# Layer 0's output projection as seven block products with streamed weight forms

## What is computed

```python
# layer 0: 6 heads of 128
q = _heads(seq_inputs @ Wq + bq)
k = _heads(seq_inputs @ Wk + bk)
v = _heads(seq_inputs @ Wv + bv)
scores = jnp.einsum('bhqd,bhkd->bhqk', q, k) / np.sqrt(HEAD_SIZE)
probs = jax.nn.softmax(scores + bias, axis=-1)      # bias: 0 or -9e15 by adj
ctx = jnp.einsum('bhqk,bhkd->bhqd', probs, v)
return ctx @ Wf + bf
# layer 1: 12 heads of 64, logits from tanh(h), leaky, masked, softmax
h = jnp.einsum('bnd,ade->bane', feat_in, W)
feat_out = jax.nn.elu(jnp.einsum('banm,bame->bane', attn, h) + b)
gate = jax.nn.sigmoid(feat_in @ H_w.T + H_b)
return gate * feat_out + (1.0 - gate) * feat_in
```

## Time and profile before

| What | Value |
|---|---|
| Median of 3 runs | 2498.94 us |
| Profiled execution, span from its first to its last instruction | 2497.4 us |
| PE busy | 2466.8 us, 99% |
| DVE busy | 1987.7 us, 80% |
| ACT, POOL busy | 922.8 us (37%), 785.2 us (31%) |
| One iteration of the loop (Q0 at 1149.84 us to the next Q0 at 1226.06 us) | 76.22 us |
| HBM read and written | 67.03 MB, 25.17 MB |

### The profile page before, as it was taken

How to read it: one execution, slowest core, us unless ns; L and a number is a source line. 1 busy time by engine, 2 the same in 40 slices (tenths; PEclk the granted TensorE clock), 3 DMA queues, 4 the chain that set the end, 5 groups by cost and what they waited for, 6 DMA issues and landing times.

```text
span 2497.4 us, 54938 instructions
## 1 busy us (share of the span) xinstructions
PE 2466.8 (99%) x22921; PEld 1765.1 (71%) x22952; DVE 1987.7 (80%) x2748; ACT 922.8 (37%) x1146; POOL 785.2 (31%) x558
## 2 busy tenths in 40 slices
PE   7999999999999999999999999999999999999997
PEld 6676677776777766777766777667777667776676
DVE  7878878778777788787787777887877877778868
ACT  6433333233333333333343333333333433333334
POOL 0133332333332333323333323333233333233331
PEclk9999999999999999999999999999999999999999
DMA  7344343343343443433433434434434334344332
GB/s 260 90 83 78 75 94 84 74 95 69 82 101 73 85 79 76 92 85 74 93 71 80 101 76 82 81 75 90 87 77 88 73 79 101 76 82 82 76 65 52
DMA packets 544290, 214.66 MB, mean 86 GB/s; under 512 B 509825, under 2 KB 519041, under 8 KB 544257
## 3 DMA queue, kind: packets, MB, share of 16 engines
q1 hardware_dynamic: 544256, 214.18, 39.8%
HBM read 67.03 MB, written 25.17 MB: 37 GB/s over the span
## 4 chain that ended last, share of the span: by engine, by line
PE 95%; DVE 3%; ACT 1%; issue 1%; DMA 0%; POOL 0%; SPq 0%; DVEq 0%; ACTq 0%; POOLq 0%
PE pair_prj L613 58%; PE pair_prj L637 29%; PE pair_att L653 3%; PE pair_att L734 2%; PE pair_att L750 1%; PE pair_att L793 1%; DVE w_lo L1005 1%; DMA arena<-in_L_gnn_Wq 0%; PE pair_prj L663 0%; ACT w_hi L1580 0%; PE pair_prj L779 0%; DVE w_top L967 0%; ACT w_lo L1615 0%; DVE arena L1055 0%; DVE p_place L1326 0%
## 5 line engine op out<-in xcount | busy, mean ns | idle before, releaser
L613 PE MATMUL pair_prj<-w_hi,arena 128*128 128x512 f16 (+1 forms) x6168 | 1445.5, 325 | 0.9 <-DVE w_lo L1005 0.9
L613 PE MATMUL pair_prj<-w_lo,arena 128*128 128x512 f16 (+1 forms) x3084 | 1002.8, 325 | 0.0
L613 PEld LDWEIGHTS pair_prj<-w_hi,arena 128*128 128x128 f16 x6168 | 603.4, 98 | 398.6 <-DVE w_lo L1005 1.0
L637 PE MATMUL pair_prj<-arena,w_hi 128*128 128x256 f16 x4536 | 747.8, 273 | 1.0 <-issue 1.0
L637 PE MATMUL pair_prj<-arena,w_lo 128*128 128x256 f16 x2268 | 618.2, 273 | 0.0
L637 PEld LDWEIGHTS pair_prj<-arena,w_hi 128*128 128x128 f16 x4536 | 439.6, 98 | 51.4 <-issue 1.4
L613 PEld LDWEIGHTS pair_prj<-w_lo,arena 128*128 128x128 f16 x3084 | 301.8, 98 | 192.7
L1911 POOL TENSOR_TENSOR rstd<-var_eps,minus_half 128x2 f32<-128x2 f32 x62 | 62.1, 1002 | 652.0 <-DVE var_eps L1024 645.0
L637 PEld LDWEIGHTS pair_prj<-arena,w_lo 128*128 128x128 f16 x2268 | 221.9, 98 | 25.7
L1930 POOL TENSOR_TENSOR arena<-arena,b_row 128x768 f32<-128x768 f32 x60 | 108.4, 1807 | 331.3 <-DVE arena L1092 331.3
L1584 ACT ACTIVATE h_hi<-arena,shift,rstd 128x768 f16<-128x768 f32 x124 | 120.7, 1020 | 218.4 <-DVE shift L1029 218.4
(11 more groups left out here) (216 smaller groups left out, 2866.1 us busy)
## 6 DMA issues: line engine op xcount, KB each, us to landing
arena<-in_x SPq DMA_DIRECT2D x63, 768.0 KB, 4.3
out<-arena SPq DMA_DIRECT2D x64, 384.0 KB, 2.3
arena<-arena SPq DMA_TRANSPOSE x372, 3.3
arena<-in_L_gnn_Wq SPq DMA_DIRECT2D x2, 1152.0 KB, 8.8
arena<-in_L_gnn_Wk SPq DMA_DIRECT2D x2, 1152.0 KB, 12.0
w_hi<-in_L_gnn_Wv SPq DMA_DIRECT2D x2, 1152.0 KB, 12.7
w_lo<-in_L_gnn_Wf SPq DMA_DIRECT2D x2, 1152.0 KB, 12.3
arena<-in_L_gnn_H_w SPq DMA_DIRECT2D x2, 1152.0 KB, 8.0
```

The lines of the kernel that those rows point to most:

```text
L613: mm = nc.tensor.matmul(pair[:, lo:hi], lhs(a, k), weight(m, k, b)[:, lo:hi], start=(k == 0 and n == 0), stop=(k == KT - 1 and n == 2))
L637: mm = nc.tensor.matmul(pair[:, c * 256:(c + 1) * 256], weight(m, k, a)[:, o:o + P], (ht0_hi, ht0_lo)[b][:, k, :], start=(k == 0 and n == ...
```

## The change

For groups 2 to 30 (`seven(g)`), the output projection of a group is no longer two products of 128 rows by 768 x 768 but one product of 256 rows, cut into 2 x 2 blocks of 128 rows by 384 features, with 384 x 384 blocks of the weight. A scheme of Strassen's kind gives it in seven block products instead of eight. Each product is 9 matmuls of 384 moving columns (three k, three float16 passes).

- Three products take blocks of the context as they are; four take sums of blocks: DVE makes four sums (`whole_sums`), ACT their high parts (`high_sums`), DVE their low parts (`low_sums`).
- Seven weight forms (three blocks of Wf, and T1 to T4, sums of blocks) are made in the first two iterations and stored in DRAM (`forms`). Of Wf's place in SBUF four slots are left; T2 stays in slot 3, and the other six forms are loaded for each group: three early in the iteration (`next_forms`), three as products 0, 1 and 2 release their slots (`late_forms`).
- The products share PSUM: 0, 3, 5 and 6 add up in `pair_prj[0][0:384]`, 2 and 4 in `pair_prj[0][512:896]`, 1 is in `pair_prj[1]`. After each product, DVE adds the running value to one quarter of `x1` (`add_form`), and the next product on the same place waits for it.
- The next Q goes to `pair_att` instead of `pair_prj`, so it waits no more for `x1`; attend(0) and attend(1) wait for Q's readout, K0 for all of `x1`.
- The statistics of `x1` are moved on DVE behind `p1_low(1)` and the readout of Q0. On POOL the bias of `x1` is added between and after `products`.

```diff
+        def seven(g):
+            return not isinstance(g, int) or 2 <= g <= GROUPS - 2
...
+                def form_product(g, n):
...
+                    elif n == 3:
+                        pe.wait_ge(sum_lo_made, 4 * (g - 2) + 2)
+                        pe.wait_ge(x1_ready, before + 1)
+                    elif n == 4:
+                        pe.wait_ge(ct_ready, 2 * g + 2)
+                        pe.wait_ge(x1_ready, before + 3)
+                    elif n == 5:
+                        pe.wait_ge(sum_lo_made, 4 * (g - 2) + 3)
+                        pe.wait_ge(x1_ready, before + 4)
+                    else:
+                        pe.wait_ge(sum_lo_made, 4 * (g - 2) + 4)
+                        pe.wait_ge(x1_ready, before + 6)
...
+                    for k in range(3):
+                        for q, (a, b) in enumerate(((0, 0), (0, 1), (1, 0))):
+                            w = slot(n % 4, b)[:, k * QUARTER:(k + 1) * QUARTER]
...
+                def late_forms():
+                    for n, form in enumerate((T4, T1, B22)):
+                        after_held(sp, transposes_held, f_psum, f_before(i) + 1 + n)
+                        load_form(n, form, slot_landed[n])
...
-                        after(pe, x1_ready, 2 * i - 1)
-                        project_columns(WQ, 0, pair_prj[0], q_psum)
-                        after(pe, x1_ready, 2 * i)
-                        project_columns(WQ, 1, pair_prj[1], q_psum)
...
+                            pe.wait_ge(z_ready, 2 * i - 3)
+                        project_columns(WQ, 0, q_pair(i, 0), q_psum)
...
                 if last:
+                    pe.wait_ge(q_ready, 2 * i + 1)
                     attend(0)
...
+                if now and seven(i):
+                    add_form(i, 0)
+                    last_context_low()
+                    add_form(i, 1)
+                    leak_and_mask(0, lambda: add_form(i, 2))
+                    low_sums(0, 3)
+                    shift1(0, lambda: add_form(i, 3))
+                    add_form(i, 4)
+                    leak_and_mask(1, lambda: add_form(i, 5))
+                    low_sums(3, 4)
+                    add_form(i, 6)
+                    shift1(1)
+                    p1_low(0, j)
+                    sum_and_invert(0, j)
```

More of the change, by code:

```diff
@@ L592, in one @@
                     transpose_rows(0, 1, ht0_lo, i + 1)
+                if first:
+                    for form in (T1, T3, T2):
+                        sp.wait_ge(weight_hi, made_high(TERM, form))
+                        store_form(form, 0, t_high[form])
+                if seven(i):
+                    late_forms()
                 if mid:
                     first_probabilities(j, j + 1)
+                if second:
+                    sp.wait_ge(forms_stored, TERMS_STORED)
+                    for form, (kh, nh) in ((B11, (0, 0)), (B12, (0, 1)), (B21, (1, 0)), (B22, (1, 1))):
+                        for part in range(2):
+                            store_form(form, part, quarter_of((w_hi, w_lo)[part][:, WF], kh, nh))
             steps(sp, one)
@@ L939, in one @@
                     logits()
-                if now:
+                if now and seven(i):
+                    for n in range(7):
+                        form_product(i, n)
+                elif now:
                     project_output(0)
@@ L1298, in leak_and_mask @@
                         .then_inc(leaky_ready, 1)
+                    if between is not None:
+                        between()
                     after_alone(dve, eye_made, leaky_ready, n)
@@ L1542, in one @@
                     context_low(0)
+                if now and seven(i):
+                    for n in (0, 2, 1, 3):
+                        whole_sums(n)
                 if mid:
                     spread_over_heads(0)
-                if now:
+                if now and not seven(i):
                     context_low(1)
@@ L1555, in one @@
                     shift1(1)
-                if nxt:
+                if nxt and not seven(i):
                     keep_x1(0)
@@ L1855, in one @@
                     h_parts(1)
+                if now and seven(i):
+                    context_parts()
+                if mid:
                     gate_tanh(0)
-                if now:
+                if now and not seven(i):
                     context_high(0)
@@ L2002, in one, with add_output_bias @@
                     add_h(1, p)
+                def add_output_bias(t):
+                    if t == 0:
+                        pool.wait_ge(x1_loaded, DMA * (i + 1))
+                    if t == 0 and first:
+                        pool.wait_ge(bf_folded, 1)
+                    nc.gpsimd.tensor_tensor(x1[:, t, :], x1[:, t, :], bf_row[:], ALU.add).then_inc(bf_added, 1)
+                early = now and seven(i)
                 if mid:
@@ L2011, in one @@
                     if not nxt:
-                        nc.gpsimd.memset(gaps_in(end_flat), 0.0).then_inc(end_gaps, 1)
-                if now:
-                    pool.wait_ge(x1_loaded, DMA * (i + 1))
-                    if first:
-                        pool.wait_ge(bf_folded, 1)
-                    for t in range(T):
-                        nc.gpsimd.tensor_tensor(x1[:, t, :], x1[:, t, :], bf_row[:], ALU.add).then_inc(bf_added, 1)
+                        nc.gpsimd.memset(gaps_in(end_flat), 0.0).then_inc(end_cleared, 1)
+                if now and not early:
+                    add_output_bias(0)
+                    add_output_bias(1)
+                if first:
+                    sum_term(T2, term_of[T2], term_of[T1], 2)
+                    sum_term(T4, term_of[T4], term_of[T2], 3)
                 if now and not nxt:
```

304 lines of the change are left out of this document (270 added, 34 removed).

## The result

The changed kernel takes 2778.86 us (median of 4 runs, 2774.55 to 2779.32); the kernel before, run beside it, 2499.11 us (2498.16 to 2499.76). The ratio is 1.112, with a 95% interval from 1.110 to 1.113. The forecast was 2747 us in a range from 2650 to 2810, so sign, case and range held, and the point was 32 us low. The profiled execution took 2774.55 us, with a span of 2772.7.

What follows compares the result with a forecast made beforehand. PE, busy 99%, bounds the kernel. 29 x (1.94 products + 4.7 wait at attend(1) + 1.7 clock) = 242, and 6 for first groups, give 248 us on the 2497.4 span; median 1.5 above: 2747 us, range 2650 to 2810.

Steps and rivals of the forecast that it cites:

- The products: From the first product to Q0: waits for DVE make each group 1.94 us longer, not 1.47 us shorter.
- P6's wait: Before the seventh product: PE idle 2.69 us for the last low sum, which follows the masked copy on DVE.
- P5's: Before the sixth product: PE idle 0.72 us, waiting for add 3 on DVE.
- The stated bound: At the seventh product: 0.3 us later if register work adds 0.05 us to each of the seven adds.
- The chain to attend(1): Before attend(1): late statistics of `x1` delay the low probabilities' transposes of t = 1; PE idle 4.7 us a group.
- The clock: At attend(1): the idle stretch makes the granted clock fall once a group, costing 1.7 us.
- P6's gap: Before the seventh product: no fall of the clock was taken for the 2.69 us of idle PE.
- The first groups: Making the forms before the loop: 6 us, DVE's work, between 0 and 15 us.
- The streamed forms: Loads of weight forms for each group: they cost nothing, hidden by the late DVE.
- One sign named for it: In the changed profile's products: no product waits for a form.
- "up to 0.2 us": At the sixth and seventh products: the wait for forms if DVE were not late.
- The rival "faster": At the seventh product and `p1_low(0)`'s transposes: DVE keeps up and PE has its saving, 2462 us; chance 0.04.

Runs made afterwards that it cites:

- e2: The changed kernel with the last low sum and the sixth add on DVE ahead of leak and masked copy of t = 1; 2726.84 us.
- e1: The changed kernel with statistics and shift of `x1` back at the head of DVE's iteration, ahead of `p1_low(1)` and Q0's readout; 2579.97 us.
- e3: The changed kernel with 40 matmuls of 256 columns, their result unread, filling PE's idle time between K0 and attend(1); 2740.57 us.
- e7: The changed kernel with Q0 and Q1 writing `pair_prj` again, so that they wait for `x1`; 2778.58 us.
- e4: The changed kernel with the weight forms loaded once, for the first group that uses them, later groups computing with stale forms; 2776.0 us.
- e6: From e1: products ordered 0, 1, 3, 2, 5, 4, 6, T3 kept for T2, DVE's and SP's work reordered to suit; 2506.16 us.
- e8: e6 with the streamed forms loaded only once, later groups computing with the forms in the slots; 2480.96 us.
- e9: e6 with a form's two parts on separate semaphores and matmuls ordered high x high, low x high, high x low; 2486.03 us.

## Why the prediction was right, step by step

- **The products: 1.94 forecast, 2.21 measured** (13.91 less 11.70). P6's wait was forecast at 2.69 us with 29 times, and the trace has 2.74 in 29 groups, ended by the low sum as forecast; e2 takes this wait away. P5's was forecast at 0.72 and is 0.59. The term that was too small is the hand-over from DVE to P6. The additions take 0.53 us from issue to issue and 0.62 in all, where the rows of `ct_lo` gave 0.47 and 0.55, but the masked copy, issued for 0.95 us where 1.0 was taken, gives part of it back, and the last low sum is done 12.21 us behind P0's start for a forecast of 12.13. P6 starts at 12.45, 0.24 us behind that end, where 0.04 was taken (from the end of add 3 to P5 it is 0.06). The stated bound, 0.3 us more at P6, came true by its size alone: it was given for register work at the additions, and what takes the 0.24 us no run shows.
- **The chain to attend(1): wait 4.7 forecast, 4.76 in the row shown, 4.79 in the mean of 29.** Its place, its releaser and the start of the statistics (forecast 10.1 behind Q0, measured 9.98) came out. From Q0 to attend(1) it is 23.66 us for 23.4, 4.93 more than before. e1 changes this order of DVE alone, and the wait goes.
- **The clock: 1.7 forecast, 1.92 measured** (8.87 less 6.95). The size came from the one fall that the trace of before had the earlier trace rows, and e3 confirms it by taking the fall at that place away. For P6's gap I had said none, and in the changed kernel that holds in 28 of 29 groups; but e3 (19 of 29 groups) and e7 (5 of 29) show that the gap is able to make the clock fall, so that was luck: I could give no reason for it. The Trainium skill (TensorE: Matmul & The Clock Gate, HAM oscillation — how this bites in real kernels) has each long enough gap of a loop paid in every round. For the 4.76 us this holds here, in all 29 groups; for the 2.74 us the same gap falls in some rounds and not in others.
- **The first groups: 6 forecast, 12 measured.** The spans differ by 275.3 us; 29 x 9.08 are 263.3, which leaves 12.0. The forecast counted DVE's work on forms and no fall of the clock, but PE waits for DVE at three places there, where it had no wait before:

```profile
73.61 0.61 PE L752 MATMUL pair_prj<-w_hi,arena 128*128 128x512 f16 x1 [2.18 <-DVE arena L1446]
...
101.76 0.39 PE L776 MATMUL pair_prj<-arena,w_hi 128*128 128x256 f16 x2 [2.19 <-DVE arena L1255]
...
109.82 0.39 PE L776 MATMUL pair_prj<-arena,w_hi 128*128 128x256 f16 x2 [2.00 <-DVE arena L1255]
```

  These are 6.4 us. Behind the first and the third of them the granted clock falls to 0.50, from about 73.5 to 76.9 us and from about 111.1 to 114.5; in its first groups the kernel before has only the one fall of the earlier trace rows, and the changed kernel has that one too, from 63.4 us. By the size that the prediction took for such a fall, two are 3.4 us more, an estimate. That makes 9.8 of the 10.6 us by which the first product of group 2 (234.18 us) starts later than O0 of that group (223.54). The last 1.4 us lie behind the loop, where attend(1) waits 5.76 us once.
- **The streamed forms: nothing forecast**, and e4 shows 3 us. One sign named for it failed: no product was to wait for a form, but P5 does in 8 of the 29 groups. Against its 0.59 us elsewhere these waits are 1.6 us longer in all, and P6, which waits for DVE behind it, then waits nearly as much less. The reason given, that the late DVE hides the loads, is confirmed by e6 and e8. Its size was not: "up to 0.2 us" at two products was taken from the landing time of one load of 768 KB, 4.3 us. The low part lands 4.8 us after its own issue and is issued 0.4 us behind the high part. By that, e6's products take 1.08 us a group more than e8's, 31 us, of which the view of waits counts 19.2, and all of the gain is gone.
- Together: 0.27, 0.23 and 0.22 us too little in each of 29 groups, 21 us, and 6 in the first groups. Of the remaining 5 us 4.3 are the distance of the profiled execution, 2774.55, from the median.
- The rival "faster" put its point of decision at P6 and at the transposes of `p1_low(0)`, and priced it at 2462 us. Both places were right; e9 removes both and gets 2486, because of the forms, which that rival had not priced, and of the first groups, which it had at 6 us for 12.

## What to carry to other kernels

Fewer multiplications on the busiest engine are a saving only if the next engine can follow: here 1.47 us of matmuls a group went for additions that DVE had to place between the instructions that the next stage was waiting for, and the order of the work alone (DVE's instructions, the products, SP's transposes and the two parts of a form) decided between +280 and -12 us. Price an instruction that is moved back by what is queued behind it on its own engine, through to the last transfer of that chain. And when a slow engine hides a transfer, price the transfer as if it were not hidden, pair by pair and from the release of its slot: it is the bound of the next version.

## What the runs showed that I had not expected

- The same idle time of PE, 2.7 us between the same matmuls, lowered the clock in 1, 2, 5 and 19 of 29 groups of four kernels (the changed one, e1, e7, e3) that differ only elsewhere in the iteration. In e1 the two groups are known by a clock of 0.63 and 0.66 in the microsecond read and by 79.7 us for 78.4. What decides it is open; no run tried to move it.
- A fall does not have one price. At P6 it is 1.14 us in e3 and 1.3 in e1 and e7, at attend(1) 1.9 in the changed kernel. In e2 the price at attend(1) changes from group to group: from one attend(1) to the next it takes in turn 83.05 and 84.21 us, all along the loop. Around attend(1) at 1189.20 us the clock of e2 is at 0.50 from about 1187.7 to 1194.6, around the next, at 1273.22, from about 1273.1 to 1276.5. So the 1.7 us that the forecast took from a single fall was near the truth for the changed kernel, and could as well have been off by a microsecond.
- Taking a wait away where the clock falls is worth more than the wait: e1 removed 138.5 us of waits and gained 199.
- The addition onto `x1` from PSUM (L1490) took 0.62 us for 384 columns and was issued every 0.53; the low sum of the same size (L1472) took 0.55.
